# A four-block transformer on one core: the projection with activations in two 16-bit parts, and the front of a fifth chunk of tokens inside the attention

## The chip, the cores and the metric

The kernel runs on one core of one Trainium2 chip. The metric is the device time of the whole kernel in microseconds, the median of three runs.

## The reference, cut to what matters

The input is x of shape (4, 2048, 256), in 32-bit floats. Four blocks follow each other, each as x = x + layernorm(block(layernorm(x))):

```python
# block 1: softmax attention, 16 heads of 16, no projections (q, k: x times a row each)
attn = softmax(q @ k.T / 4) @ x_head
# block 2: mixes each token with the one ahead of it, then
out = sigmoid(xr @ W_r.T) * (square(relu(xk @ W_k.T)) @ W_v.T)
# block 3: linear attention with 8 heads, then its own MLP
x = x + msg;  x2 = layernorm(x, g2, be2)
h = gelu(x2 @ w1.T + b1)              # exact gelu, 1024 wide
x = x + (h @ w2.T + b2)               # the projection that the change is about
# block 4: gated MLP, 768 wide, integer weights
h = silu(x @ wg.T) * (x @ wu.T);  out = h @ wd.T
```

## The kernel before, in words

**Attention.** The first part of the program (`softmax_attention`) goes through 64 pairs of batch and head, called heads 0 to 63 here, eight of them to a group. A head is 16 key blocks j. For each, TensorE makes the scores (L468, 16-bit), ScalarE takes their exponential (L742, two instructions of 128x1024 a key block), and TensorE multiplies them with the values (L591). Scores are made three key blocks ahead, in three buffers of PSUM. At a head's end VectorE copies the sums out of PSUM (L894), and TensorE turns them (L641).

**The front inside the attention.** The tokens are handled in 16 chunks of 512 behind the attention, four chunks to a batch. Block 2 and the first half of block 3 of a chunk (norms, mixing, three matrix products of block 2, then k, v, q and the sums k times v of block 3) are its front. The fronts of the first `EARLY` = 4 chunks are done during the attention, from head 17 on, when the heads of batch 0 are there. A front is 17 pieces on TensorE (`PIECES`, two transposes of n, mix_r0 ... val1, two of u, k0 ... q1, kv), spread over steps, 18 to a chunk. Each piece uses the one spare bank of PSUM, is cut in two parts that stand three key blocks apart, and is read by VectorE before the next one may begin. `front_at` says behind which key blocks of a head pieces stand: at j = 2 in every head, and at j = 10 as well in odd heads and in the last group. So 68 pieces stand in heads 18 to 63: 23 heads hold two, 22 hold one. ScalarE does three extra instructions a chunk between its exponentials (L681, L684, L687), POOL (GpSimd) the inverse roots of the norms, and SyncE (SP) the loads and stores.

**The later layers.** `later_layers` does the rest as a pipeline over chunks. A stage of each chunk belongs to one of eight streams, and stream s works on chunk "iteration minus SHIFT[s]". Streams 0, 1 and 2 are the front of the chunks from `EARLY` on; l and m make the message of the linear attention and y; a does fc (L1514, y times w1, 48 products in 16 bits a chunk), the gelu (L1646, ScalarE, into hT in 32 bits) and the projection (L1378 with hT, 32 products in 32 bits a chunk, called proj0 to proj3); b the integer MLP's gate and up products (L1542) and the down products (L1558); c the output. Iterations 1 and 2 ("thin") hold 0, 1, 2, l and m alone; from iteration 3 on a is there, and from then to iteration 12 an iteration does all ("full"); in iteration 13 stream 2 is the last of the front's, and 14 to 20 are "drain". The order on each engine is written out by hand in `PE_ORDER`, `ACT_ORDER`, `DVE_ORDER`, `POOL_ORDER` and `SP_ORDER`, one list of stages for each phase. Engines take their queues in that order and wait on semaphores. PSUM banks 0 and 1, 2 and 3, 4 and 5 are shared between stages of different streams; 6 and 7 hold fc's products and the projection's. fc's product i waits until the gelu has read product i - 2 (`gelu_done`).

The lines that turn up below: `stats` and `norm` helpers L1744 to L1755 (VectorE), POOL's inverse root L1344 and its sum with the bias b2 L1354, x4's residual sum L1893, the transposes and splitting of w1 at L1450, L1705, L1708 and L1826, and VectorE's and ScalarE's two instructions for the parts of the gated product, L1920 and L1688.

## Time and profile before

| | us |
|---|---|
| median of three runs (3086.8 to 3090.0) | 3089.66 |
| the profiled execution | 3088.71 |
| its span, first to last instruction | 3086.4 |
| TensorE busy in it | 2866.7 |
| ScalarE busy | 2412.6 |
| VectorE busy | 1374.1 |

The span is what the profile accounts for; the profiled execution's own time lies 2.3 us above it. Busy times are sums over the whole span, and the two parts of the program have different limits, so the stretches have to be read one by one. The attention ends at about 1981 us.

### The profile page before, as it was taken

The page shows a single profiled execution, that of the slowest core. Times are in us where ns is not written, and L with a number is a line of the kernel's source. Part 1 is how long each engine was busy: PE and PEld are TensorE (multiplying, and loading weights), DVE is VectorE, ACT ScalarE, POOL GpSimd, SP SyncE. Part 2 cuts the span into 40 slices and gives each one's busy share as a digit, 9 for nine tenths or more (in the row PEclk, how much of TensorE's full clock was granted, in tenths as well). Part 3 has the DMA queues.
Part 4 walks back from the last instruction along what each step waited for, and adds up shares of the span by engine and source line. Part 5 has one row for each costly group of instructions (what it writes and reads, how often), then busy time and mean ns, then how long its engine had stood idle before and what let it go on. Part 6 is the DMA issues. An engine that isn't in the chain of part 4 may idle for free. (4 is left out here: it accounts for less than half of the span.)

```text
span 3086.4 us, 48514 instructions
## 1 busy us (share of the span) xinstructions
PE 2866.7 (93%) x18320; PEld 1153.1 (37%) x18320; DVE 1374.1 (45%) x3395; ACT 2412.6 (78%) x2681; POOL 223.8 (7%) x193
## 2 busy tenths in 40 slices
PE   3999999999999999999999999779999999999996
PEld 0221221222222222222222222256766666666664
DVE  5221220321432233223330142277778888865675
ACT  5999999999999999999999999654444444443432
POOL 0000000000000000000000000011111111211110
PEclk9999999999999999999999999889999999999998
DMA  3411111311210211111120111121222212111110
GB/s 119 153 36 37 64 39 37 100 43 33 76 57 25 83 62 55 52 50 40 59 74 25 37 52 43 39 75 55 63 82 68 61 61 76 61 48 51 38 48 22
DMA packets 125586, 177.51 MB, mean 58 GB/s; under 512 B 42248, under 2 KB 100616, under 8 KB 125128
## 3 DMA queue, kind: packets, MB, share of 16 engines
...
## 5 line engine op out<-in xcount | busy, mean ns | idle before, releaser
L742 ACT ACTIVATE probs<-ps 128x1024 f32<-128x1024 f32 x2048 | 1893.0, 1168 | 46.5 <-PE ps L468 45.7
L591 PE MATMUL ps<-probs,vals 128*32 128x512 f32 x8192 | 1092.2, 605 | 2.9 <-ACT probs L742 2.9
L468 PE MATMUL ps<-qT,kT 64*128 64x512 f16 x4096 | 728.4, 385 | 83.8 <-DMA kT<-split_dram 17.9
L468 PEld LDWEIGHTS ps<-qT,kT 64*128 64x128 f16 x4096 | 173.2, 93 | 1125.4 <-ACT probs L742 1030.8
L1680 ACT ACTIVATE gate<-layers_ps 128x512 f32<-128x512 f32 x96 | 57.3, 597 | 279.4 <-PE layers_ps L1542 157.4
L894 DVE COPY sums<-ps 128x512 f32<-128x512 f32 x64 | 44.3, 692 | 516.8 <-PE ps L591 516.8
L591 PEld LDWEIGHTS ps<-probs,vals 128*32 128x32 f32 x8192 | 161.5, 108 | 294.1 <-issue 228.8
L1378 PE MATMUL layers_ps<-weight_mem,hT 128*128 128x256 f32 x1024 | 230.8, 380 | 0.0
L1378 PEld LDWEIGHTS layers_ps<-weight_mem,hT 128*128 128x128 f32 x1024 | 193.0, 190 | 29.9 <-ACT hT L1646 1.2
L1514 PE MATMUL layers_ps<-yT,weight_mem 128*128 128x512 f16 x768 | 172.8, 379 | 13.6 <-ACT hT L1646 13.6
L1542 PE MATMUL layers_ps<-n4T,weight_mem 128*128 128x512 f16 x768 | 177.3, 384 | 6.7 <-DVE y_out L1755 4.3
L1646 ACT ACTIVATE hT<-layers_ps,weight_mem,fc_scale 128x512 f32<-128x512 f32 x128 | 95.3, 772 | 44.6 <-PE layers_ps L1514 44.4
L813 DVE TENSOR_SCALAR qk<-ps,q_factor 128x512 f32<-128x512 f32 x32 | 24.0, 750 | 223.3 <-PE ps L459 223.2
L1514 PEld LDWEIGHTS layers_ps<-yT,weight_mem 128*128 128x128 f16 x768 | 73.9, 98 | 100.4 <-ACT hT L1646 18.1
L1542 PEld LDWEIGHTS layers_ps<-n4T,weight_mem 128*128 128x128 f16 x768 | 75.8, 99 | 95.3 <-issue 11.5
L1913 DVE SCALAR_TENSOR_TENSOR gate<-layers_ps,gate 128x512 f32<-128x512 f32 x96 | 66.3, 690 | 68.5 <-PE layers_ps L1542 59.3
L1558 PE MATMUL layers_ps<-weight_mem,gated 128*128 128x256 f16 x768 | 88.1, 273 | 3.2 <-DVE gated L1920 3.2
L1378 PE MATMUL layers_ps<-weight_mem,uT 128*128 128x256 f32 x384 | 85.1, 379 | 0.6 <-issue 0.6
L1344 POOL TENSOR_TENSOR rstd_x<-ve_x,neghalf_k 128x4 f32<-128x4 f32 x55 | 62.9, 1144 | 294.0 <-DVE ve_x L1750 293.5
L1558 PEld LDWEIGHTS layers_ps<-weight_mem,gated 128*128 128x128 f16 x768 | 74.8, 98 | 18.5 <-issue 7.3
L1378 PEld LDWEIGHTS layers_ps<-weight_mem,uT 128*128 128x128 f32 x384 | 72.9, 190 | 12.0 <-issue 1.3
L1688 ACT ACTIVATE gated<-gate 128x512 f16<-128x512 f32 x96 | 60.0, 625 | 18.7 <-DVE gate L1913 18.6
...
## 6 DMA issues: line engine op xcount, KB each, us to landing
...
```

Of the source, the lines that this page charges most:

```text
L468: last = nc.tensor.matmul(SCORES[slot][:, n * BANK:(n + 1) * BANK], kT[buf][rows, j * P:(j + 1) * P], qT[buf][rows, q0:q0 + BANK], start=T ...
L591: mm = nc.tensor.matmul(ACC[32 * c:32 * c + 32, :], vals[buf][:, j, :], probs[:, j % PROBS, c * BANK:(c + 1) * BANK], start=(j == 0), stop ...
L742: nc.scalar.activation(probs[:, j % PROBS, half * T // 2:(half + 1) * T // 2], SCORES[slot_of(at)], ACT.Exp, scale=OPERAND_SCALE ** -2).th ...
L1344: pool.tensor_tensor(rstd[l][:, :], ve[l][:, :], neghalf[:, :], ALU.pow).then_inc(sem("rstd_" + l), 1)
L1378: last = nc.tensor.matmul(dst, x[:, k, blk * P:(blk + 1) * P], w[:, k, :], start=(k == 0), stop=(k == kk - 1))
L1514: last = nc.tensor.matmul(ps[:, 6 + i % 2, :], w1_parts[:, w, k, i * P:(i + 1) * P], yT16[:, y, k, :], start=((w, y, k) == products[0]), s ...
L1542: last = nc.tensor.matmul(ps[:, a + i, :], W16[w][:, k, m * P:(m + 1) * P], n4T16[:, p, k, :], start=(p == k == 0), stop=(p == 1 and k == ...
L1558: last = nc.tensor.matmul(dst, gated16[:, p, k, blk * P:(blk + 1) * P], W16["wd"][:, k, :], start=(p == k == 0), stop=(p == 1 and k == M2 ...
L1646: A(hT[:, i, :], ps[:, 6 + i % 2, :], ACT.Gelu, scale=fc_scale[:, i:i + 1], bias=W["b1"][:, 0, i:i + 1]).then_inc(sem("gelu_done"), 1)
L1680: A(gate[:, m % 2, :], ps[:, up_bank(m), :], ACT.Silu, scale=DEQUANT / NORM_SCALE if exact16 else DEQUANT).then_inc(sem("silu_done"), 1)
L1688: A(gated16[:, 0, m, :], gate[:, m % 2, :], ACT.Copy).then_inc(sem("gated_high"), 1)
L1913: V.scalar_tensor_tensor(dst, ps[:, up_bank(m) + 1, :], DEQUANT / NORM_SCALE * HIDDEN_SCALE if exact16 else DEQUANT, gate[:, m % 2, :], AL ...
```

## The change

**The projection.** hT now holds the activations in two 16-bit parts. ScalarE's gelu writes to a new tile `hidden` of four slots; a second ScalarE instruction for each of the eight blocks (stages hh0 to hh3, two blocks each) scales it and writes the high part; a VectorE instruction (hl0 to hl3) writes what is left of it as the low part and counts `h_done`. w2 is split in two 16-bit parts as well, by VectorE during the last group of the attention (`rows_of_fc`, with one more reduction over partitions on POOL). A block of the projection is then 24 products in 16 bits (high by high, high by low, low by high) in place of 8 in 32 bits. It waits for `h_done`, and the gelu waits for `h_done` too, three blocks back, because of the four slots. The orders of all engines are written anew for this.

**The fifth chunk.** `EARLY` is 5, and `front_at` gives (2, 10) for every head. 85 pieces stand in heads 18 to 62: two in each of them, except one in 19, 21 and 62 and none in 23. `SHIFT` changes with it: LEAD falls from 1 to 0, and the pipeline of the later layers has iterations 0 to 19, of which 0 holds the load of the message's input and the diagonal copy alone, 1 is the only thin one, 2 to 11 are full, 12 has stream 2 as the last of the front's, and 13 to 19 are drain. Splitting w1 and the integer weights moves into iteration 1. To make room, the tiles attn and x0 are laid over n1 and x1, so the next chunk's loads wait for `mix_mm`, `n1_done` and `x1_kept`.

```diff
@@ constants and the front's places
-EARLY = 4
+EARLY = 5
 def front_at(head):
-    return (2, 10) if head // GH + 1 == GROUPS or head % 2 else (2,)
+    return (2, 10)
@@ rows_of_fc (VectorE, last group)
+                if e == 3:
+                    fch.link(V.tensor_tensor(w2, w2, hidden_bound[:, :].unsqueeze(2).broadcast_to([P, M1, C]), ALU.mult))
+                    fch.link(V.tensor_reduce(widest_row[:, 0:1], w2.rearrange("p m c -> p (m c)"), AX.X, ALU.max, apply_absolute_value=True))
...
+                    fch.link(V.tensor_scalar(product, w2[:, m, :], widest_row[:, 0:1], PROJ_SCALE, ALU.mult, ALU.mult))
+                    fch.link(V.tensor_copy(parts[:, :, 0, :], product))
+                    fch.link(V.tensor_tensor(parts[:, :, 1, :], product, parts[:, :, 0, :], ALU.subtract))
@@ orders, one list of each engine's
 ACT_ORDER "all":
-fc0 mix fc1 fc2 uT mix_k fc3 nT mix_r up0 up1 high0 up2 high1 up3 high2 up4 high3 up5 high4 keep high5 ...
+fc0 hh0 mix fc1 fc2 hh1 uT fc3 mix_k hh2 nT keep hh3 mix_r up0 high0 up1 up2 high1 high2 up3 up4 high3 up5 high4 high5 ...
 POOL_ORDER "drain":
-x4 ffn b2 msg o
+b2 x4 ffn msg o
@@ later_layers
-        attn = sb("attn", [P, H, K4, D])
+        attn = fr_a[:, :, :].rearrange("p k c -> p (k c)").rearrange("p (h k d) -> p h k d", h=H, k=K4)
-        f = r_gate
+        x0, f = x1, r_gate
-        hT = sb("hT", [P, M1, N])
+        hT, hidden = sb("hT", [P, M1, N]), sb("hidden", [P, 4, N])
@@ load_in (SP)
                 sp.wait_ge(sem("x1_done"), c)
+                sp.wait_ge(sem("mix_mm"), c)
...
+                sp.wait_ge(sem("n1_done"), c)
+                sp.wait_ge(sem("x1_kept"), c)
@@ proj (TensorE)
-                    pe.wait_ge(sem("gelu_done"), c * M1 + M1)
-                    tok_out(blocks(6)[:, k, :], hT, k, W["w2"], M1).then_inc(sem("proj_mm"), 1)
+                    pe.wait_ge(sem("h_done"), c * M1 + M1)
+                    products = [(h, w, m) for h, w in ((0, 0), (0, 1), (1, 0)) for m in range(M1)]
+                    for h, w, m in products:
+                        last = nc.tensor.matmul(blocks(6)[:, k, :], h_parts[:, h, m, k * P:(k + 1) * P], w2_parts[:, w, m, :],
+                                                start=((h, w, m) == products[0]), stop=((h, w, m) == products[-1]))
+                    last.then_inc(sem("proj_mm"), 1)
@@ fc and h_high (ScalarE)
                     for i in range(part * M1 // 4, (part + 1) * M1 // 4):
                         act.wait_ge(sem("fc_mm"), c * M1 + i + 1)
-                        A(hT[:, i, :], ps[:, 6 + i % 2, :], ACT.Gelu, scale=fc_scale[:, i:i + 1], bias=W["b1"][:, 0, i:i + 1]).then_inc(sem("gelu_done"), 1)
+                        act.wait_ge(sem("h_done"), c * M1 + max(i - 3, 0))
+                        A(hidden[:, i % 4, :], ps[:, 6 + i % 2, :], ACT.Gelu, scale=fc_scale[:, i:i + 1], bias=W["b1"][:, 0, i:i + 1]).then_inc(sem("gelu_done"), 1)
...
+                        A(h_parts[:, 0, i, :], hidden[:, i % 4, :], ACT.Copy, scale=hidden_scale[:, i:i + 1]).then_inc(sem("h_high"), 1)
@@ h_low (VectorE)
+                        V.scalar_tensor_tensor(h_parts[:, 1, i, :], hidden[:, i % 4, :], hidden_scale[:, i:i + 1], h_parts[:, 0, i, :],
+                                               ALU.mult, ALU.subtract).then_inc(sem("h_done"), 1)
@@ o_layer (VectorE)
-                V.tensor_tensor(flat(o), wide(6, 2), flat(o), ALU.add).then_inc(sem("o_done"), 1)
+                V.scalar_tensor_tensor(flat(o), wide(6, 2), proj_scale[:, 0:1], flat(o), ALU.mult, ALU.add).then_inc(sem("o_done"), 1)
```

What the new orders do is seen in the order of the built programs. In the rows below, L numbers of the changed program are its own.

**TensorE, from the transposes of iteration 2 (before) to the first fc.** Before, iteration 1 stands ahead of these rows; L1366 turns n (fr_a), u and y, L1495 is the message, L1372 and L1378 are products in 32 bits, L1450 turns w1, L1514 is fc:

```order
L1366 MATMUL layers_ps<-ident,u 128x128 x8
L1495 MATMUL layers_ps<-kv_diag,q_in 128x132 x8
L1372 MATMUL layers_ps<-uT,weight_mem 128x512 x4
L1378 MATMUL layers_ps<-weight_mem,uT 128x256 x8
L1372 MATMUL layers_ps<-xk,weight_mem 128x512 x4
L1378 MATMUL layers_ps<-weight_mem,xr 128x256 x8
L1378 MATMUL layers_ps<-weight_mem,k_act 128x256 x8
L1450 MATMUL layers_ps<-ident,weight_mem 128x128 x8
L1378 MATMUL layers_ps<-weight_mem,uT 128x256 x8
L1366 MATMUL layers_ps<-ident,y 128x128 x8
L1484 MATMUL layers_ps<-v_ones,k_feat 128x130 x8
L1514 MATMUL layers_ps<-yT,weight_mem 128x512 x12
```

The changed program, from its very first instruction in the later layers to the first fc:

```order
L1483 MATMUL layers_ps<-ident,weight_mem 128x128 x8
L1395 MATMUL layers_ps<-ident,fr_a 128x128 x8
L1528 MATMUL layers_ps<-kv_diag,q_in 128x132 x8
L1407 MATMUL layers_ps<-weight_mem,xr 128x256 x8
L1483 MATMUL layers_ps<-ident,weight_mem 128x128 x8
L1401 MATMUL layers_ps<-xk,weight_mem 128x512 x4
L1407 MATMUL layers_ps<-weight_mem,k_act 128x256 x8
L1395 MATMUL layers_ps<-ident,y 128x128 x8
L1547 MATMUL layers_ps<-yT,weight_mem 128x512 x12
```

The products with uT (q, v and k) and v_ones of an iteration are gone ahead of the first fc, and so is a whole round of transposes, xk, xr and k_act. Both halves of w1 are turned in the one iteration that is left.

**ScalarE, in a full iteration, from the first gelu.** hT and hidden are the gelu's outputs, n1T, xk and xr belong to the mixing, uT to u:

```order
L1646 ACT_TABLE_LOAD
L1646 ACTIVATE hT<-layers_ps,weight_mem,fc_scale 128x512 x2
L1585 ACTIVATE n1T<-layers_ps 128x2x512
L1591 ACTIVATE xk<-n1T,one_minus_mu 128x512 x2
L1591 ACTIVATE xr<-n1T,one_minus_mu 128x512 x2
L1646 ACTIVATE hT<-layers_ps,weight_mem,fc_scale 128x512 x4
L1609 ACTIVATE uT<-layers_ps,weight_mem 128x512 x2
L1601 ACTIVATE k_act<-layers_ps 128x1024
L1603 ACTIVATE k_act<-k_act 128x1024
L1646 ACTIVATE hT<-layers_ps,weight_mem,fc_scale 128x512 x2
L1654 ACTIVATE n4T<-layers_ps 128x1024
L1596 ACTIVATE r_gate<-layers_ps 128x1024
```

The changed program:

```order
L1682 ACTIVATE hidden<-layers_ps,weight_mem,fc_scale 128x512 x2
L1691 ACTIVATE hT<-hidden,hidden_scale 128x512 x2
L1622 ACTIVATE n1T<-layers_ps 128x2x512
L1628 ACTIVATE xk<-n1T,one_minus_mu 128x512 x2
L1628 ACTIVATE xr<-n1T,one_minus_mu 128x512 x2
L1682 ACTIVATE hidden<-layers_ps,weight_mem,fc_scale 128x512 x4
L1691 ACTIVATE hT<-hidden,hidden_scale 128x512 x2
L1646 ACTIVATE uT<-layers_ps,weight_mem 128x512 x2
L1682 ACTIVATE hidden<-layers_ps,weight_mem,fc_scale 128x512 x2
L1638 ACTIVATE k_act<-layers_ps 128x1024
L1640 ACTIVATE k_act<-k_act 128x1024
L1691 ACTIVATE hT<-hidden,hidden_scale 128x512 x2
```

Two copies of the high part (hT<-hidden) now stand between the first two gelus and the mixing, and two more after the sixth gelu.

**VectorE, in the first iteration that does x4, from x4's statistics on.** x4's end is ve_x, n4T is the low part of the next transposed input, r_gate is f:

```order
L1750 TENSOR_SCALAR ve_x<-mv_x 128x4
L1785 SCALAR_TENSOR_TENSOR xk<-n1T,weight_mem,xk 128x512 x2
L1785 SCALAR_TENSOR_TENSOR xr<-n1T,weight_mem,xr 128x512 x2
L1788 TENSOR_SCALAR n1T<-n1T,keep 128x2
L1755 TENSOR_SCALAR n<-x,mv_x,rstd_x 128x256 x4
L1744 BN_STATS stats_attn<-attn 128x6 x4
L1748 BN_AGGR mv_attn<-stats_attn 128x2 x4
L1750 TENSOR_SCALAR ve_attn<-mv_attn 128x4
L1903 SCALAR_TENSOR_TENSOR n4T<-layers_ps,n4T 128x1024
L1793 SCALAR_TENSOR_TENSOR r_gate<-r_gate,layers_ps 128x1024
```

The changed program:

```order
L1795 TENSOR_SCALAR ve_x<-mv_x 128x4
L1930 SCALAR_TENSOR_TENSOR hT<-hidden,hidden_scale,hT 128x512 x2
L1830 SCALAR_TENSOR_TENSOR xk<-n1T,weight_mem,xk 128x512 x2
L1830 SCALAR_TENSOR_TENSOR xr<-n1T,weight_mem,xr 128x512 x2
L1833 TENSOR_SCALAR n1T<-n1T,keep 128x2
L1930 SCALAR_TENSOR_TENSOR hT<-hidden,hidden_scale,hT 128x512 x2
L1800 TENSOR_SCALAR n<-x,mv_x,rstd_x 128x256 x4
L1956 SCALAR_TENSOR_TENSOR n4T<-layers_ps,n4T 128x1024
L1930 SCALAR_TENSOR_TENSOR hT<-hidden,hidden_scale,hT 128x512 x4
L1838 SCALAR_TENSOR_TENSOR r_gate<-r_gate,layers_ps 128x1024
```

Eight low parts (hT<-hidden,hidden_scale,hT) stand in three places, the statistics of attn go behind f, and the last four low parts stand behind n4T.

## Rows read from the trace of the kernel before

**Rows 1.** the page: span, and busy tenths of three engines in 40 equal slices
```profile
span 3086.4 us, 48514 instructions
...
PE   3999999999999999999999999779999999999996
...
DVE  5221220321432233223330142277778888865675
ACT  5999999999999999999999999654444444443432
```

**Rows 2.** windows in the attention: head 14, heads 17-63, head 40, 41, 31, 56-63
```profile
core 0: us, PE busy (x) PEld busy (x) DVE busy (x) ACT busy (x) POOL busy (x), PEclk, DMA share, GB/s
469.98:499.31 29.33, 27.60 (x198) 5.92 (x196) 1.57 (x5) 29.33 (x34) 0.00 (x0) 1.00 0.10 32
558.44:1978.58 1420.14, 1375.00 (x9728) 336.87 (x9726) 416.38 (x885) 1400.75 (x1514) 34.74 (x33) 1.00 0.16 52
1248.59:1278.31 29.72, 28.94 (x210) 7.14 (x206) 12.14 (x23) 29.17 (x32) 0.00 (x0) 1.00 0.18 60
1278.31:1309.03 30.72, 30.59 (x218) 8.47 (x218) 8.35 (x15) 30.23 (x34) 0.00 (x0) 1.00 0.17 57
975.28:1007.59 32.31, 30.59 (x210) 7.50 (x210) 3.75 (x7) 31.36 (x35) 0.00 (x0) 1.00 0.09 32
1735.34:1978.58 243.24, 236.87 (x1672) 59.87 (x1668) 69.73 (x140) 237.70 (x256) 8.61 (x6) 1.00 0.12 39
```

**Rows 3.** groups by line: work of a front piece on TensorE
```profile
L516 PE MATMUL ps<-weight_mem,fr_xr 128*128 128x256 f32 x128 | 36.2, 405 | 0.0
L560 PE MATMUL ps<-fr_uT,weight_mem 128*128 128x512 f32 x32 | 18.0, 645 | 0.0
```

**Rows 4.** windows in the later layers, from one first fc matmul to the next
```profile
2020.70:2062.80 42.10, 33.03 (x144) 26.62 (x145) 35.17 (x103) 18.06 (x20) 6.14 (x7) 0.82 0.26 75
2062.80:2121.60 58.80, 53.38 (x251) 39.73 (x249) 38.79 (x124) 21.24 (x25) 10.36 (x9) 0.97 0.28 81
2473.60:2544.40 70.80, 68.41 (x355) 48.38 (x353) 57.74 (x158) 33.44 (x43) 12.89 (x10) 1.00 0.22 67
2864.50:2909.80 45.30, 43.94 (x242) 29.64 (x240) 32.01 (x86) 18.92 (x25) 6.36 (x5) 1.00 0.13 46
```

**Rows 5.** groups by line: the projection, down products, high and low halves
```profile
L1378 PE MATMUL layers_ps<-weight_mem,hT 128*128 128x256 f32 x1024 | 230.8, 380 | 0.0
L1558 PE MATMUL layers_ps<-weight_mem,gated 128*128 128x256 f16 x768 | 88.1, 273 | 3.2 <-DVE gated L1920 3.2
L1688 ACT ACTIVATE gated<-gate 128x512 f16<-128x512 f32 x96 | 60.0, 625 | 18.7 <-DVE gate L1913 18.6
L1920 DVE TENSOR_TENSOR gated<-gate,gated 128x512 f16<-128x512 f32 x96 | 65.5, 686 | 14.3 <-ACT gated L1688 12.8
```

**Rows 6.** timelines (start us, us long) of TensorE and VectorE at the start of the later layers
```profile
1988.51 1.94 PE L1366 MATMUL layers_ps<-ident,fr_a 128*128 128x128 f32 x8 [8.53 <-issue]
2009.97 1.22 DVE L1793 SCALAR_TENSOR_TENSOR r_gate<-r_gate,layers_ps 128x1024 f32<-128x1024 f32 x1 [4.78 <-PE layers_ps L1378]
2029.93 0.17 DVE L1859 TENSOR_SCALAR denom<-layers_ps 128x16 f32<-128x16 f32 x1 [0.54 <-PE layers_ps L1495]
2060.01 2.28 DVE L1826 TENSOR_TENSOR weight_mem<-gated,weight_mem 128x2048 f16<-128x2048 f32 x1
2062.85 1.43 PE L1514 MATMUL layers_ps<-yT,weight_mem 128*128 128x512 f16 x5
```

**Rows 7.** timeline of TensorE in a full iteration
```profile
2482.95 5.35 PE L1514 MATMUL layers_ps<-yT,weight_mem 128*128 128x512 f16 x24 [1.05 <-ACT hT L1646]
```

**Rows 8.** timelines of VectorE and GpSimd: x4's sum, in the full iteration, then drain
```profile
2478.55 3.37 DVE L1893 TENSOR_TENSOR x<-x_in,x 128x1024 f32<-128x1024 f32 x1
2478.48 2.35 POOL L1354 TENSOR_TENSOR o<-x,row_mem 128x1024 f32<-128x1024 f32 x1 [4.89 <-DVE x L1755]
...
2867.26 1.23 DVE L1893 TENSOR_TENSOR x<-x_in,x 128x1024 f32<-128x1024 f32 x1
```

141 lines of the change are left out of this document (88 added, 53 removed).

## The prediction, made before the changed kernel was run

> **What bounds the kernel now.** I read the page's slices first, to see that the program has two parts [rows 1]. In the first 25 or so of the 40 slices TensorE and ScalarE are both at nine tenths or more; behind them TensorE alone is, with VectorE at seven to eight tenths and ScalarE at four. So each part needs its own table by stretches.
>
> In the attention a window is one head, from one copy of the sums to the next [rows 2]. Head 14, with no piece of the front, takes 29.33 us, and ScalarE is busy for all of it: its 32 exponentials set the pace, while TensorE has 29.33 - 27.60 = 1.7 us to spare. Head 40, with one piece, takes 29.72 us with TensorE busy for 28.94. Head 41, with two, takes 30.72 with TensorE busy for 30.59: it has become the bound. Over heads 17 to 63 the time is 1420.1 us, and 47 heads of 29.33 would be 1378.5: the 68 pieces cost 41.6 us.
>
> In the later layers a window is one iteration, from its first fc product to the next one's [rows 4]. A full iteration takes 70.8 us with TensorE busy for 68.4 and VectorE for 57.7; one of the drain takes 45.3 with TensorE busy for 43.9, VectorE for 32.0. TensorE bounds both; VectorE idles 13.1 and 13.3 us.
>
> **The change, part by part.**
>
> *Front in the attention.* Twenty-two heads with a single piece cost about 0.39 each (head 40), 8.6 in all. The other 41.6 - 8.6 = 33.0 us belong to the 23 heads with two: 1.43 each. Now 41 heads hold two and three hold one: 41 x 1.43 + 3 x 0.39 = 59.8 us, which is **18 us more**. The eight last heads have stood next to each other with two pieces already (one only in head 63): 243.24 - 8 x 29.33 = 8.6 us for 15 pieces, 1.15 a pair, so pairs in neighbouring heads don't pile up there. That is the low end: 48 us, a rise of 7. The dearest pair (head 31, 32.31 us) cost 2.98; 41 of them would be 122 us, a rise of 81. I take 1.43, since it is the mean of 23 cases and lies near head 41's. The fifth chunk's work is far more than that: 12 of a chunk's 17 pieces stand in four groups, two of 36.2 us and two of 18.0 for four chunks, one of each shown [rows 3], so 27 us a chunk, and most of it lies in TensorE's spare time. VectorE's new instructions for w2 stand in the last group of heads, where it is busy for 69.7 of 243.2 us [rows 2], and go at nothing. They handle some ten times 128x1024, and at x4's 1.23 us each [rows 8] they would be 12 us if that cover were gone.
>
> *A thin iteration less.* Before, TensorE's first instruction in the later layers is at 1988.5 and the first fc at 2062.85 [rows 6], 74.3 us for two iterations in which TensorE idles much; the second takes 42 us [rows 4]. The changed order on TensorE has one such iteration left. In it VectorE is the chain, up to w1's low part, which fc needs. In the old second iteration VectorE is busy for 35.2 us [rows 4]; of that n2, u, q_feat, k_feat and the last norm of n1 (some 6.5 us, at 1.2 to 1.4 for each pass over 128x1024) now stand behind the low part or are gone, which leaves 28.7. The old window idles for another 6.9; I keep half, 3.3. Ahead of it TensorE needs 6.5 us for w1, n and the message, the last of them 3.1 at the clock of these iterations (its granted share is 0.82 there [rows 4]); the old order let mixing and message overlap with other work, as the heads of f, of the message and of the low part show [rows 6]. That is 38.5 us to the first fc. 74.3 - 38.5 = 36; I take **35 us less**, with 28 and 40 as ends. The exponential and splitting work of the dropped iteration is the fifth chunk's and is hidden in the attention, as priced above.
>
> *The projection on TensorE.* A chunk's 64 records of the 32-bit product take 230.8/1024 x 64 = 14.4 us by the group and 13.8 by start times; 96 in 16 bits, at the down product's 88.1/768 = 0.115 (0.108 by start times), take 11.0 or 10.4 [rows 5]. That is 3.4 us less a chunk.
>
> *What it adds elsewhere.* Per chunk eight copies on ScalarE (0.625 us, like L1688) and eight two-input instructions on VectorE (0.69, like L1920; 0.62 from start to start in a row), 5.0 us each [rows 5]. In a full iteration VectorE has 57.7 + 5.0 = 62.7 us to do, 65.4 with the waits inside its norm chains, and TensorE 68.4 - 3.4 = 65.0: they are **level**, so a full iteration cannot fall by 3.4. I walked one with these durations. The first joint is fc's: the gelu of product 4 comes 1.25 us later, because two copies of the high part stand ahead of the mixing on ScalarE, so fc2 waits some 2.3 us where it waited 1.05 [rows 7]. The second is at n4: the last low parts and n4_low sit close behind each other, and f and the first up product wait half a microsecond. The third is k_feat, where VectorE waits for ScalarE's exponential and then keeps kv, q and the next fc behind it. The walk closes at 68.4 us: **2.4 less**, for nine iterations that hold streams a and 1 in full, 21.6 us.
>
> In the drain TensorE has 43.9 - 3.4 = 40.5 us of work. The projection now waits for the last low part: eighth gelu, two copies of 0.6, two low parts of 0.6, where it waited for nothing; about 1.6 us of the gain go there. A further one is POOL's. In a full iteration x4's sum takes 3.37 us while POOL adds b2 (2.35 us) beside it, and 1.23 in the drain, where POOL does so later [rows 8]. The new order puts b2 first in the drain too, so x4's sum grows by 2.1 us there and hands some 1 us on to the low parts and the projection. The Trainium skill says the same (GPSIMD Engine Reference, its table's row on SBUF interfaces: shared with VectorE, contention with instructions that have two SBUF inputs); the trace agrees by these two rows. By that rule the low parts, with two SBUF inputs, would be slowed as well wherever they meet b2. Without any such meeting the drain would be 4 us shorter in all than I say. I take 43.6 us an iteration, **1.7 less**, for four: 6.8. The iteration with a but no b saves 2.5, the one with stream 2 last 2.3, and the last chunk's 1.5. Together the 16 projections save 21.6 + 6.8 + 6.3 = **34.7 us**, of 54 that TensorE's work alone would give. SP's new waits cost nothing: the attn load now starts behind the transpose of n, some 4 us into an iteration, and is wanted after 30; x0's is wanted after 60. Without that cover, a load's 5.5 to 6.4 us.
>
> **The sum.** Span: 3086.4 + 18 - 35 - 34.7 = 3034.7 us; the profiled execution's own time 3088.71 - 51.7 = 3037.0, and the median of the runs stands 0.95 above it: 3038.
>
> **The rivals.**
> - *TensorE stays the bound throughout*: VectorE's 13 us of idle time swallow the 5.0 whole. 16 x 3.4 = 54 instead of 34.7: 3019. For it is that the idle time is there; against it, that VectorE waits only where it must.
> - *VectorE binds and the full iterations gain nothing*: 21.6 us less of gain, 3060. For it: 65.4 us of chain in 70.8 leave little, and the queue is strictly in order, so each wait for POOL's roots adds.
> - *Slower: VectorE keeps all its waits.* They are for POOL, ScalarE and TensorE and may simply shift. A full iteration is then 57.7 + 5.0 + 13.1 = 75.8 us, 5.0 more, and the drain's 50.3; with 5 us more in 16 iterations, 80 in place of a gain of 34.7, the time is 3038 + 115 = 3153. It ends slower as soon as an iteration is longer by (35 - 18)/16 = 1.1 us on average. Against it: most of these waits are for TensorE, whose work shrinks.
> - *Pairs pile up in the attention*, each as dear as head 31's: 63 us more, 3101. It takes 2.7 us a pair to lose all the gain. Against it are the last eight heads.
> - *The change doesn't shorten the pipeline's start*: some other chain (the late loads, the 8 us of copies for the integer weights on ScalarE) holds the first fc for 15 us more: 3053.
>
> **How the numbers follow.** Forecast 0.58; TensorE bound throughout 0.11; full iterations without gain 0.16; a late start 0.07; piled pairs 0.04; VectorE's waits kept 0.03; 0.01 for something else. About 0.2% (6 us) is what a measurement of this kernel can tell from no change. All cases but the two slower ones are over 6 us faster: faster 0.91, within 0.2% 0.02 (either slow mechanism half way), slower 0.07. Low end: TensorE bound with the low price of the front, near 3010; I cut at 3014. High end: no gain in full iterations, with a few microseconds more in the attention: 3064. Outside lie about 0.15.
>
> **What would show it.** Right: heads with two pieces at 30.5 to 31 us, and the last head's sums at about 1997 instead of 1978.6; the first fc near 2046 (18 later, 35 earlier); full iterations at 68.4 with VectorE busy for about 63; the drain at 43.6; x4's sum near 3.4 in the drain. Wrong: full iterations at 67.4 or below with TensorE never waiting (first rival), or at 70.8 and more with TensorE waiting for VectorE (second and third), heads at 32 (fourth), or a first fc past 2060 (fifth).

## The result, and the profile after

Over its runs the changed kernel takes 3069.12 us (median of 4, 3066.76 to 3071.46), the kernel before 3089.18 (3086.8 to 3090.0): a ratio of 0.9936, 95% interval 0.9924 to 0.9948. It is faster by 20 us. The forecast was 3038 with 3014 to 3064 as its range, so the direction was right and the size was not. The profiled execution took 3067.5 us, its span is 3065.7.

The page of the changed kernel, span and the same three rows of the 40 slices as in [rows 1]:

```profile
span 3065.7 us, 50078 instructions
...
PE   3999999999999999999999999958999999999996
...
DVE  5221230323433432433241152157998989976886
ACT  5999999999999999999999999954455555554543
```

In the last 14 slices VectorE went from seven and eight tenths to eight and nine, and ScalarE from four to five. TensorE still shows nines. The slices don't tell which of the two is waited for.

Windows of the changed kernel, with the columns of [rows 2]: heads 17 to 63, head 40, the first iteration with fc, a full one, the first drain iteration and the third:

```profile
559.14:1991.63 1432.49, 1394.05 (x9840) 349.70 (x9838) 467.65 (x995) 1407.20 (x1517) 40.30 (x39) 1.00 0.17 54
1259.31:1290.01 30.70, 30.42 (x210) 6.80 (x208) 13.61 (x27) 29.85 (x33) 1.11 (x1) 1.00 0.36 100
...
2041.90:2106.60 64.70, 54.90 (x280) 38.22 (x281) 45.86 (x132) 30.86 (x35) 11.39 (x10) 0.89 0.21 65
2523.60:2593.60 70.00, 65.38 (x387) 45.36 (x385) 62.99 (x165) 38.29 (x52) 13.16 (x11) 1.00 0.22 67
2792.00:2842.70 50.70, 44.60 (x275) 27.90 (x273) 40.49 (x95) 25.81 (x35) 6.87 (x5) 0.93 0.19 63
2889.70:2935.00 45.30, 41.05 (x275) 26.64 (x273) 39.37 (x94) 23.44 (x33) 6.86 (x5) 1.00 0.14 46
```

Read against [rows 2] and [rows 4]:

| stretch (iterations cut at their first fc product) | before | after | difference | forecast |
|---|---|---|---|---|
| to the last head's sums | 1978.6 | 1991.6 | +13.0 | +18 |
| from there to the first fc product | 84.3 | 50.3 | -34.0 | -35 |
| the first iteration with fc | 58.8 | 64.7 | +5.9 | -2.5 |
| the ten after it, to the drain | 697.0 | 685.4 | -11.6 | -23.9 |
| four iterations of the drain | 183.0 | 189.7 | +6.7 | -6.8 |
| last chunk, to the end | 84.8 | 84.0 | -0.8 | -1.5 |
| from the first fc product to the end | 1023.6 | 1023.8 | **+0.2** | **-34.7** |

The two parts of the change at the front came out nearly as priced. The projection in two parts gained nothing: TensorE's work in a full iteration fell by 3.0 us where 3.4 were forecast (68.41 to 65.38), VectorE's rose by 5.25 (57.74 to 62.99), and the iteration fell from 70.8 us to 70.0 only. TensorE, which waited for 2.4 us of an iteration, now waits for 4.6.

What it waits for in that full iteration, from the view of waits (engine, line, releaser: us in total, times, longest):

```profile
PE layers_ps L1395 <- DVE n L1800: 1.3, 1, 1.3
PE layers_ps L1547 <- ACT hidden L1682: 1.2, 1, 1.2
PE layers_ps L1395 <- DVE q L1880: 1.1, 1, 1.1
...
PE layers_ps L1407 <- DVE y_out L1800: 0.8, 1, 0.8
```

The second and the third were there before ([rows 7] has one). The first and the last are new: TensorE waits for VectorE's norm of n4, and mix_r then waits for y_out's norm to give banks 4 and 5 back.

### The profile page after: what moved, and what is told of

Its sections match the earlier page's. It is cut to its first block and busy times, and to the rows that moved or that the text cites. A ratio compares the mean times of both kernels' runs of the same rounds, so it can differ in the third digit from the quotient of the medians.

```text
span 3065.7 us, 50078 instructions
## 1 busy us (share of the span) xinstructions
PE 2820.9 (92%) x18832; PEld 1101.8 (36%) x18832; DVE 1491.9 (49%) x3565; ACT 2481.5 (81%) x2796; POOL 233.4 (8%) x194
## 5 line engine op out<-in xcount | busy, mean ns | idle before, releaser
L471 PE MATMUL ps<-qT,kT 64*128 64x512 f16 x4096 | 719.2, 385 | 74.7 <-DMA kT<-split_dram 18.9
L1547 PE MATMUL layers_ps<-yT,weight_mem 128*128 128x512 f16 x768 | 181.3, 390 | 31.7 <-ACT hidden L1682 20.9
L1557 PE MATMUL layers_ps<-weight_mem,hT 128*128 128x256 f16 x1536 | 180.4, 277 | 11.1 <-DVE hT L1930 11.1
L1557 PEld LDWEIGHTS layers_ps<-weight_mem,hT 128*128 128x128 f16 x1536 | 152.2, 99 | 37.8 <-DVE hT L1930 12.3
L1682 ACT ACTIVATE hidden<-layers_ps,weight_mem,fc_scale 128x512 f32<-128x512 f32 x128 | 94.3, 771 | 56.5 <-PE layers_ps L1547 34.7
L1930 DVE SCALAR_TENSOR_TENSOR hT<-hidden,hidden_scale,hT 128x512 f16<-128x512 f32 x128 | 89.1, 746 | 22.4 <-ACT hT L1691 22.4
L1691 ACT ACTIVATE hT<-hidden,hidden_scale 128x512 f16<-128x512 f32 x128 | 84.9, 712 | 2.0
```

The costliest lines, as they stand in the source:

```text
L471: last = nc.tensor.matmul(SCORES[slot][:, n * BANK:(n + 1) * BANK], kT[buf][rows, j * P:(j + 1) * P], qT[buf][rows, q0:q0 + BANK], start=T ...
L1547: last = nc.tensor.matmul(ps[:, 6 + i % 2, :], w1_parts[:, w, k, i * P:(i + 1) * P], yT16[:, y, k, :], start=((w, y, k) == products[0]), s ...
L1557: last = nc.tensor.matmul(blocks(6)[:, k, :], h_parts[:, h, m, k * P:(k + 1) * P], w2_parts[:, w, m, :], start=((h, w, m) == products[0]), ...
L1682: A(hidden[:, i % 4, :], ps[:, 6 + i % 2, :], ACT.Gelu, scale=fc_scale[:, i:i + 1], bias=W["b1"][:, 0, i:i + 1]).then_inc(sem("gelu_done"), 1)
L1691: A(h_parts[:, 0, i, :], hidden[:, i % 4, :], ACT.Copy, scale=hidden_scale[:, i:i + 1]).then_inc(sem("h_high"), 1)
L1930: V.scalar_tensor_tensor(h_parts[:, 1, i, :], hidden[:, i % 4, :], hidden_scale[:, i:i + 1], h_parts[:, 0, i, :], ALU.mult, ALU.subtract). ...
```

## The loop behind the full iteration

From these waits I formed **theory A**, of which the expectations below speak. An iteration's length is set neither by TensorE's work nor by VectorE's, but by a loop made of stretches of both:

1. VectorE works with no gap above 0.4 us from k_feat to the norm of y_out (k_feat, y_low, in1, kv, diag, in2, q_feat, x4, the first two pairs of low parts, mix, ffn, n4, y_out).
2. That norm frees banks 4 and 5 for TensorE's mix_r; from mix_r on TensorE works without a gap to the end of v and k.
3. ScalarE takes the k features (one pass, a table, one exponential), and VectorE's k_feat follows.

The projection's products stand in stretch 2, and half of its new low parts (hl0, hl1) in stretch 1. So the change takes from the one and gives to the other. The joints, in timelines (start us, us long): first VectorE and TensorE in the kernel before,

```profile
2465.42 1.23 DVE L1831 SCALAR_TENSOR_TENSOR k_feat<-layers_ps,k_feat 128x1024 f32<-128x1024 f32 x1
2490.68 1.90 DVE L1755 TENSOR_SCALAR y_out<-layers_ps,mv_ffn,rstd_ffn 128x256 f32<-128x256 f32 x4
2492.72 3.69 PE L1378 MATMUL layers_ps<-weight_mem,xr 128*128 128x256 f32 x16
2536.21 1.23 DVE L1831 SCALAR_TENSOR_TENSOR k_feat<-layers_ps,k_feat 128x1024 f32<-128x1024 f32 x1
```

then the same in the changed kernel, with the start of v and k:

```profile
2515.46 1.23 DVE L1876 SCALAR_TENSOR_TENSOR k_feat<-layers_ps,k_feat 128x1024 f32<-128x1024 f32 x1 [1.12 <-ACT k_feat L1666]
2543.22 1.90 DVE L1800 TENSOR_SCALAR y_out<-layers_ps,mv_ffn,rstd_ffn 128x256 f32<-128x256 f32 x4
2545.26 3.69 PE L1407 MATMUL layers_ps<-weight_mem,xr 128*128 128x256 f32 x16 [0.81 <-DVE y_out L1800]
2574.89 7.07 PE L1407 MATMUL layers_ps<-weight_mem,uT 128*128 128x256 f32 x32
2585.42 1.22 DVE L1876 SCALAR_TENSOR_TENSOR k_feat<-layers_ps,k_feat 128x1024 f32<-128x1024 f32 x1 [1.09 <-ACT k_feat L1666]
```

mix_r starts as y_out's norm ends, in both kernels: 2490.68 + 1.90 = 2492.58 and 2543.22 + 1.90 = 2545.12. The loop set the pace of the kernel before as well, but only just: TensorE's wait at this joint was too short to be listed, and experiment 2 shows that its own way from k_feat to mix_r was 0.3 us shorter than VectorE's. Cut at these starts, the stretches are, in one full iteration of each (the runs of the lower rows come below):

| kernel | k_feat to mix_r | mix_r to v, k | v, k to k_feat | sum |
|---|---|---|---|---|
| before | 27.30 | 32.96 | 10.53 | 70.79 |
| changed | 29.80 | 29.63 | 10.53 | 69.96 |
| b2_late | 27.67 | 30.12 | 10.53 | 68.32 |
| diag_moved | 28.82 | 29.65 | 10.53 | 69.00 |
| more_in | 32.59 | 31.06 | 10.53 | 74.18 |
| more_out | 29.68 | 31.31 | 10.54 | 71.53 |
| fifth_only | 27.28 | 32.95 | 10.53 | 70.77 |
| before_b2_late | 27.02 | 34.02 | 10.53 | 71.57 |
| best | 27.28 | 30.32 | 10.53 | 68.13 |

The three columns add up to the iteration whatever bounds it, because they are cuts of it. What can speak for A is which column an edit moves, and by how much.

The change took 3.3 us from the second column and put 2.5 into the first. Two more things stood in the first column already: x4's sum, 3.4 us because GpSimd adds b2 beside it, and diag. So A says where gain is to be had, and the experiments try it.

## The experiments

Each line with times has the ratio to the kernel before, measured on the same chip, with its 95% interval.

**1. The two halves apart.** proj_only keeps the projection and takes the fifth chunk's front back out of the attention; fifth_only is the changed kernel with the 32-bit projection.

```diff
-EARLY = 5
+EARLY = 4
...
-    return (2, 10)
+    return (2, 10) if head // GH + 1 == GROUPS or head % 2 else (2,)
```

> The changed kernel with EARLY = 4 and front_at as before, so the projection in two 16-bit parts alone, with the new orders. Theory A (chained loop: a full iteration is VectorE's unbroken stretch from k_feat to y_out's norm, then TensorE's from mix_r to k, then 3.4 us of ScalarE; the projection takes 3.4 us from TensorE's part and adds 2.5 us of low parts to VectorE's): full iterations about 70.0 us, nothing gained over all, 3086 to 3090 us. Theory B (the projection does bring its gain, and the fifth chunk brings less than the pipeline's shorter start shows): full iterations still 70, but the whole 20 us or more faster than before, near 3065.

```diff
-                    pe.wait_ge(sem("h_done"), c * M1 + M1)
-                    products = [(h, w, m) for h, w in ((0, 0), (0, 1), (1, 0)) for m in range(M1)]
...
+                    pe.wait_ge(sem("gelu_done"), c * M1 + M1)
+                    tok_out(blocks(6)[:, k, :], hT, k, W["w2"], M1).then_inc(sem("proj_mm"), 1)
```

> The changed kernel with the projection as before (32-bit, no high and low parts, no splitting of w2), so the fifth chunk alone, with the new orders without the stages hh and hl. Theory A: the fifth chunk gives all of the gain, first fc near 2042, full iterations near 70.6, drain 45.3; 3063 to 3070 us, no slower than the changed kernel. Theory B: 3085 us or more.

fifth_only: 3068.59 us (ratio 0.9934, 0.9917 to 0.9951), the same as with the projection. The whole gain of the change is the fifth chunk's. Beside fifth_only the new projection makes the ten iterations 10 us shorter (685.4 for 695.3), the first 2.7 longer, the last chunk 1.2 shorter, and the four of the drain 7.3 longer (189.7 for 182.4). In fifth_only TensorE's granted clock is 1.00 in all four; in the changed kernel it is in one of them only.

proj_only: 3104.98 us (1.0053, 1.0036 to 1.0070), 16 us slower than before and outside what I expected. From the first fc product to the last chunk's it is 7.0 us shorter than before (931.7 for 938.7), and the last chunk 2.8 longer. The loss is in the start: the last head's sums stand within 0.7 us of before, and the first fc product comes 18.9 us later, at 2081.8 instead of 2062.85. The timeline of TensorE in proj_only shows the wait ahead of it:

```profile
2078.19 3.80 PE L1517 MATMUL layers_ps<-v_ones,k_feat 128*128 128x130 f32 x16 [17.78 <-DVE k_feat L1876]
```

The changed thin order fits one thin iteration, and proj_only has two; the k features then stand behind keep_x1 and w16's 8 us of copies. Two kernels try whether that, and not the projection, makes the start late: one moves w16 alone behind the k features, the other gives the thin iterations their orders of the kernel before.

```diff
-    "thin": "w1a mix uT v q_low q w1b mix_k mix_r yT keep_x1 w16 k_low k".split(),
+    "thin": "w1a mix uT v q_low q w1b mix_k mix_r yT keep_x1 k_low k w16".split(),
```

> The kernel with the projection's half alone (3105), with one thing changed: in ScalarE's thin order w16's 8 us of copies stand behind the k features' two passes. If the 19 us that its first fc came late were those of the start (VectorE's k_feat waited 9.2 us for the exp behind w16, and k, v and q feature work behind it), the first fc comes 5 to 15 us earlier than 2081.8 and the time is 3090 to 3100, the full iterations staying at 69.8. If the loss lay in the iterations, nothing changes: 3105.

```diff
-    "thin": "w1a mix msg uT q v mix_r w1b mix_k val k yT kv".split(),
+    "thin": "w1a mix uT msg q v mix_k mix_r val w1b k yT kv".split(),
...
-    "thin": "w1a mix uT v q_low q w1b mix_k mix_r yT keep_x1 w16 k_low k".split(),
+    "thin": "w1a w16 mix uT v q_low mix_k q mix_r w1b k_low yT k keep_x1".split(),
...
-    "thin": "diag mix msg in0 y in1 q_feat f y_low x2 k_feat w1_low kv in2 n2 u".split(),
+    "thin": "diag mix msg in0 in1 y q_feat f x2 y_low k_feat in2 w1_low n2 kv u".split(),
...
-    "thin": "msg in0 in1 f x2 n2".split(),
+    "thin": "in0 msg f in1 x2 n2".split(),
```

> The kernel with the projection's half alone, with the thin iterations' orders of the kernel before (w1's second half and w16 where they were). If its loss of 16 us is that of the start, the first fc comes at 2060 to 2068 for 2081.8, the rest stays (fc to fc 932 us), and the time is 3082 to 3092. If the projection itself costs, it stays above 3097.

proj_only_w16: 3102.69 us (1.0032, 1.0017 to 1.0047), first fc at 2077.3. That is 4.5 us earlier, less than expected: keep_x1, which waits for x2's sum, still stands ahead of the k features on ScalarE. Its five runs lie between 3091.9 and 3103.5 us, the widest of all kernels here, and the two fastest are those with the highest granted clock (0.986 and 0.985 for 0.983), so its time tells little beside its trace. proj_only_start: 3092.76 us (1.0011, 1.0002 to 1.0021), 0.8 above what I expected, first fc at 2071.4 (2060 to 2068 expected), and 932.5 us from there to the last chunk's. So 10 of the 19 us were the orders. The other 8.5 stand in proj_only_start's trace, in one wait of VectorE: diag, which the changed order puts at the head of a thin iteration, waits there for the products of the message ahead of it.

```profile
2033.70 0.18 DVE L1894 COPY kv_diag<-kv_sums 32x64 f32<-32x64 f32 x1 [8.33 <-PE layers_ps L1528]
```

In the kernel before diag stood at the end of a thin iteration, and ran without a wait. No run moves it back, so for these 8.5 us the cause is read from the trace and not tried. proj_only and proj_only_start agree on what the projection does from the first fc on in a program with the old front: 6 to 7 us less up to the last chunk, 1 to 3 more in it, 4 to 5 in all where 34.7 were forecast.

**2. b2 off the path.** In the changed kernel GpSimd's order begins with b2, which meets x4's sum in stretch 1. Here it stands behind f, and behind ffn in the drain.

```diff
-    "all": "b2 x4 ffn f msg x2 n2 o in0 in1".split(),
+    "all": "x4 ffn f b2 msg x2 n2 o in0 in1".split(),
...
-    "drain": "b2 x4 ffn msg o".split()}
+    "drain": "x4 ffn b2 msg o".split()}
```

> The changed kernel with POOL's sum with b2 put behind the root for f in full iterations and behind ffn's root in the drain, so that it no longer runs beside x4's sum. Theory A: x4's sum takes 1.23 instead of 3.37 us, and as it stands in VectorE's stretch of the loop, full iterations fall by about 2 us to 68, drain by up to 2: 3040 to 3050 us. Theory C (the limit is VectorE's total work and POOL is not in it, or the wait moves to another pair): full iterations stay within 0.5 us of 70, over 3062 us.

3058.14 us (0.9897, 0.9880 to 0.9913). x4's sum, in the timelines of VectorE in the changed kernel and of b2_late:

```profile
2528.68 3.37 DVE L1946 TENSOR_TENSOR x<-x_in,x 128x1024 f32<-128x1024 f32 x1
```

```profile
2525.47 1.23 DVE L1946 TENSOR_TENSOR x<-x_in,x 128x1024 f32<-128x1024 f32 x1
```

The sum is 2.1 us shorter, the first stretch too (29.80 to 27.67), and the full iteration 1.7, because the second stretch takes 0.5 more. By the trace b2 has a price in its new place too: it runs beside a VectorE instruction of 4 columns (L1795), which takes 0.77 us for 0.17, and TensorE waits 0.3 us for the gate product behind it. In the first two of the ten iterations stretch 1 gets no shorter (31.3 to 31.8 us and 27.1 to 27.1), and both are 0.8 us longer; in the last the clock fell (0.92 for 0.97). So the ten give only 4.1 us together (681.3 for 685.4), and the four of the drain 7.9 (181.8 for 189.7). Most of these 7.9 are the clock's and one gelu's: an iteration of the drain at a granted clock of 1.00 takes 45.3 us in the changed kernel and 44.9 here. The gain came out at 11 us where I had expected 19 to 29.

The same move in the kernel before, as a cross:

```diff
-    "all": "b2 x4 ffn f in0 x2 n2 msg o in1".split(),
+    "all": "x4 ffn f in0 b2 x2 n2 msg o in1".split(),
```

> The kernel before with POOL's sum with b2 put behind the root for attn in full iterations (the drain had it late already). Theory A: before, TensorE never waits behind x4's sum (its two waits are for q_feat and for the gelu), so full iterations stay at 70.8 within 0.3 and the time at 3089 within 3 us. If x4's sum was on the path there as well: 68.7 a full iteration, near 3070 us.

3100.73 us (1.0036, 1.0023 to 1.0048): slower, and outside my expectation. x4's sum fell to 1.22 us here as well, but b2 met another instruction. From its timelines, GpSimd, VectorE and TensorE:

```profile
2511.95 2.43 POOL L1354 TENSOR_TENSOR o<-x,row_mem 128x1024 f32<-128x1024 f32 x1
2512.70 2.81 DVE L1755 TENSOR_SCALAR x<-r_gate,mv_f,rstd_f 128x256 f32<-128x256 f32 x4
2521.20 2.04 PE L1495 MATMUL layers_ps<-kv_diag,q_in 128*128 128x132 f32 x16 [0.90 <-DVE gate L1913]
```

The norm in the middle took 1.37 us in the kernel before. The delay reaches the up products' read and the message, inside stretch 2, which is 1.1 us longer. Stretch 1 is only 0.3 us shorter (27.30 to 27.02), though x4's sum is 2.1 us shorter, so the full iteration is 71.6 us, 0.8 longer. The reason stands at the joint of this iteration, in VectorE's and TensorE's timelines of before_b2_late:

```profile
2495.84 1.90 DVE L1755 TENSOR_SCALAR y_out<-layers_ps,mv_ffn,rstd_ffn 128x256 f32<-128x256 f32 x4
2499.41 3.62 PE L1378 MATMUL layers_ps<-weight_mem,xr 128*128 128x256 f32 x16
```

y_out's norm ends at 2497.74, and mix_r starts 1.7 us later without a wait, straight behind TensorE's own products. TensorE's own way from k_feat to mix_r, its waits for q's features and a gelu included, takes 27.0 us. So in the kernel before the two ways were level within 0.3 us: a shorter VectorE stretch could give it no more than that, while new VectorE work in it would lengthen stretch 1 in full. The cross shows as well that a move of b2 has its price wherever it lands.

**3. The same work inside and outside the stretch.** Four more instructions a chunk, two behind each of hl0 and hl1 (more_in), or behind each of hl2 and hl3 (more_out, where the first line's pair is (2, 3)). spare is a tile of 128x512 in 16 bits that nothing reads:

```diff
+                    if part in (0, 1):
+                        for again in range(2):
+                            dve.wait_ge(sem("spare_done"), c * 4 + part % 2 * 2 + again)
+                            V.scalar_tensor_tensor(spare[:, :], W["akv"][:, 0, :], hidden_scale[:, 0:1], W["akv"][:, 1, :], ALU.mult, ALU.subtract).then_inc(sem("spare_done"), 1)
```

> The changed kernel with four more VectorE instructions of 512 columns a chunk (about 0.7 to 0.8 us each with its wait, some 3 us a chunk, into a tile that nothing reads), two behind each of hl0 and hl1, inside the stretch from k_feat to the norm of y_out. Theory A (a loop of two stretches, VectorE from k_feat to the norm of y_out and TensorE from mix_r to the end of k, sets the full iteration): the full iteration goes from 70.0 to about 73 us, the time by 27 to 32 us in nine to ten iterations, and by 0 to 12 in the drain: 3096 to 3112. Rival (VectorE's total work sets it): the same here. Rival (TensorE sets it, 65 us busy of 70): at most +1 an iteration, under 3080.

> The same four instructions, but behind hl2 and hl3, outside that stretch, where VectorE waits 1.5 us for TensorE's value product and 0.4 and 0.7 us around it. Theory A: the full iteration stays within 0.7 us of 70.0; in the drain, where the projection waits for hl3, up to 3 us a chunk in four chunks: 3069 to 3088. Rival (total work): full iteration about 73, as in the other kernel, 3096 to 3112.

more_in: 3110.5 us (1.0066, 1.0049 to 1.0083), full iteration 73.2 to 74.5. more_out: 3092.18 us (1.0009, 0.9999 to 1.0019), full iteration 71.5. The times stand 41 and 23 us above the changed kernel, and the second is above what A expected. VectorE's and TensorE's work is the same in both, in one full iteration of each (more_in first):

```profile
2541.80:2616.00 74.20, 67.00 (x386) 46.50 (x385) 65.73 (x169) 38.56 (x51) 13.00 (x11) 0.98 0.21 64
```

```profile
2537.50:2609.00 71.50, 66.95 (x386) 46.59 (x385) 65.75 (x169) 38.40 (x51) 13.11 (x11) 0.98 0.21 66
```

Equal work and 2.7 us of difference: total work on VectorE can't be the bound, and the place decides. The table of stretches shows where: in more_in the first column is 2.8 us longer (29.80 to 32.59), in more_out 0.1 shorter. But both have 1.4 to 1.7 us more in the second column, which A did not foresee. TensorE is busy for 1.6 us more there with the same products. mix_r's 16 matmuls take 5.38 us in more_out where they took 3.69, and the windows around them give the reason (PEclk is the third number from the end; mix_r is the second row):

```profile
2557.10:2559.00 1.90, 1.09 (x8) 0.86 (x8) 1.86 (x5) 1.87 (x3) 0.00 (x0) 1.00 0.00 0
2559.00:2564.30 5.30, 5.25 (x17) 4.32 (x18) 4.58 (x6) 4.00 (x6) 0.00 (x0) 0.68 0.00 0
```

The granted clock is 0.68 over mix_r, partly at 1.2 GHz and partly at 2.4. In the changed kernel it is 1.00 there, as this window shows:

```profile
2545.20:2548.80 3.60, 3.54 (x17) 3.15 (x18) 2.92 (x3) 3.60 (x6) 0.00 (x0) 1.00 0.00 0
```

Before both, TensorE had nearly the same waits: 1.2 to 1.3 us, the transposes of n4 (1.1 us), and 0.8 us. Taking the clock off, the four instructions cost 2.8 us inside (0.7 each), all of it in the first column. Outside they are not free either. mix_r's clock fell in four full iterations of more_out; in others it stayed at 1.00, and there TensorE waits ahead of the second up product, for 2.8 us in the first two of the ten iterations and for 0.9 in the next two. By the orders it waits for the bank that VectorE's f, now later, gives back. One of these two:

```profile
2344.93 3.69 PE L1408 MATMUL layers_ps<-weight_mem,xr 128*128 128x256 f32 x16 [0.81 <-DVE y_out L1801]
2354.74 1.89 PE L1580 MATMUL layers_ps<-n4T,weight_mem 128*128 128x512 f16 x8 [0.93 <-issue]
```

The second column is 30.82 us there, 1.2 above the changed kernel's, and the iteration 71.1. Where mix_r is slow its 1.7 us hide that wait. So the same work costs 2.8 us inside and 1.2 outside at a granted clock of 1.00: it finds some 1.6 us of room outside and none inside. The half of A that these kernels test stands, that VectorE's place decides and not its total. Its expectation for more_out, within 0.7 us of 70.0, failed by the clock and, where the clock held, by stretch 2, which is not TensorE's alone.

**4. Work moved out of the stretch, none added.** diag's small copies go from between kv and in2 to behind y_out's sum, an iteration later.

```diff
-STAGES = {"0": "load_in in0 in1 in2 keep_x1", "1": "mix mix_r mix_k val f x2 n2 u", "2": "uT k k_low k_feat v q q_low q_feat kv", "l": "load_msg diag w1a w1b w1_low w16", "m": "msg y yT y_low",
+STAGES = {"0": "load_in in0 in1 in2 keep_x1", "1": "mix mix_r mix_k val f x2 n2 u", "2": "uT k k_low k_feat v q q_low q_feat kv", "l": "load_msg w1a w1b w1_low w16", "m": "diag msg y yT y_low",
...
-    "all": "x4 hl0 mix ffn hl1 b2 n4 out n4_low hl2 hl3 f up0 in0 low0 up1 up2 low1 low2 up3 x2 msg up4 low3 y up5 low4 n2 low5 o u k_feat y_low in1 kv diag in2 q_feat".split(),
+    "all": "x4 hl0 mix ffn hl1 b2 n4 out diag n4_low hl2 hl3 f up0 in0 low0 up1 up2 low1 low2 up3 x2 msg up4 low3 y up5 low4 n2 low5 o u k_feat y_low in1 kv in2 q_feat".split(),
```

> The changed kernel with the 16 small copies of the message's block diagonal (diag, 1.4 us with the wait ahead of it) moved on VectorE from between kv and in2 to behind y_out's sum, one iteration later, where VectorE waits for the high part of n4T. No work is added or removed. Theory A (the stretch of VectorE from k_feat to the norm of y_out is a part of the loop): it is 1.4 us shorter, so the full iteration falls from 70.0 to about 68.6, and the time by 10 to 18 us: 3051 to 3059. Rival (VectorE's total work, or TensorE's, sets it): 70.0 and 3069 as before, since both are unchanged.

3063.05 us (0.9917, 0.9901 to 0.9934), full iteration 69.0. The stretch is shorter by 1.0, not 1.4, since in2 now comes ahead of GpSimd's root, in VectorE's timeline:

```profile
2519.90 1.38 DVE L1800 TENSOR_SCALAR fr_a<-fr_x,mv_x,rstd_x 128x256 f32<-128x256 f32 x4 [0.60 <-POOL rstd_x L1373]
```

6 us came of it, for 10 to 18 expected, with the same sign as A and against both rivals, by which nothing should have moved.

**5. The way down from there.** In b2_late the start still had TensorE waiting for w1's low part. b2_thin computes it ahead of f, where VectorE waited, and copies w16 ahead of keep_x1:

```diff
-    "thin": "w1a mix uT v q_low q w1b mix_k mix_r yT keep_x1 w16 k_low k".split(),
+    "thin": "w1a mix uT v q_low q w1b mix_k mix_r yT w16 keep_x1 k_low k".split(),
...
-    "thin": "diag mix msg in0 y in1 q_feat f y_low x2 k_feat w1_low kv in2 n2 u".split(),
+    "thin": "diag mix msg in0 y in1 w1_low q_feat f y_low x2 k_feat kv in2 n2 u".split(),
```

> The best version (b2_late, 3058) with the thin iteration's orders changed: VectorE computes w1_low ahead of f, in a wait of 5.4 us, and ScalarE copies w16 ahead of keep_x1, in waits. TensorE's first fc, which waited 10.8 us for w1_low, comes 5 to 7 us earlier (2036 to 2038 for 2043), and the clock may not fall there. If the first full iteration passes it on, 3050 to 3054; if it waits for the gelus or for n1 instead, 3058 as before.

3050.47 us (0.9874, 0.9857 to 0.9890), with the first fc product at 2035.7. It waits 3.8 us where it waited 10.8, in the changed kernel and then in b2_thin:

```profile
2041.94 4.74 PE L1547 MATMUL layers_ps<-yT,weight_mem 128*128 128x512 f16 x12 [10.81 <-DVE weight_mem L1871]
```

```profile
2035.72 2.75 PE L1547 MATMUL layers_ps<-yT,weight_mem 128*128 128x512 f16 x12 [3.83 <-DVE yT L1923]
```

The same 12 products take 2.75 us instead of 4.74; the clock granted over the slow ones is 0.57, so TensorE was at its 1.2 GHz level for most of them.

best adds diag's move to b2_thin, and gelu_first then takes hh0 and hl0 out of the gelus' way:

> The same move in the best version (b2_thin, 3050.5), where the full iteration is 68.3 and TensorE waits 1.17 us for q's features and 1.16 for a gelu. By A the first wait goes and the second stays or shrinks: full iteration 66.5 to 67.5, time 3036 to 3045. If TensorE's other waits take the place, 3048 to 3052.

```diff
-    "all": "fc0 hh0 mix fc1 fc2 hh1 uT fc3 mix_k hh2 nT keep hh3 mix_r up0 high0 up1 up2 high1 high2 up3 up4 high3 up5 high4 high5 v k_low k yT keep_x1 q_low q".split(),
+    "all": "fc0 mix fc1 hh0 fc2 hh1 uT fc3 mix_k hh2 nT keep hh3 mix_r up0 high0 up1 up2 high1 high2 up3 up4 high3 up5 high4 high5 v k_low k yT keep_x1 q_low q".split(),
...
-    "all": "x4 hl0 mix ffn hl1 b2 n4 out diag n4_low hl2 hl3 f up0 in0 low0 up1 up2 low1 low2 up3 x2 msg up4 low3 y up5 low4 n2 low5 o u k_feat y_low in1 kv in2 q_feat".split(),
+    "all": "x4 mix hl0 ffn hl1 b2 n4 out diag n4_low hl2 hl3 f up0 in0 low0 up1 up2 low1 low2 up3 x2 msg up4 low3 y up5 low4 n2 low5 o u k_feat y_low in1 kv in2 q_feat".split(),
```

> The kernel 'best' (3054.3, full iteration 68.1) with ScalarE's first high parts hh0 (1.3 us) moved behind the gelus of fc1, VectorE's hl0 moved behind mix with them, and in the drain diag moved behind out. In 'best' TensorE's only large wait in the full iteration is 2.2 us of fc2 for the gelus of fc1, which stand behind hh0 and n1T's five passes on ScalarE. If that wait is ScalarE's chain, the gelus come 1.2 us earlier and the full iteration is 66.8 to 67.2, the drain again 45, the time 3035 to 3045. If a slot of hidden (gelu 4 waits for hl0, now later) or n1's chain takes its place, the full iteration stays at 68 and the time is 3050 to 3054.

best: 3054.25 us (0.9888, 0.9872 to 0.9905), full iteration 68.1, above both of its expectations. The wait for q's features went, and that of fc2 for ScalarE's gelus grew from 1.2 to 2.2 us; the drain lost 3.6 us, where diag stood ahead of n4_low (gelu_first has it behind out, and still loses 1.7 of them). gelu_first: 3050.29 us (0.9874, 0.9858 to 0.9891), full iteration 68.4. The gelus of fc1 come earlier, and the next one waits instead for a slot of hidden, which hl0 now gives back later, from ScalarE's and TensorE's timelines of gelu_first:

```profile
2523.55 1.45 ACT L1682 ACTIVATE hidden<-layers_ps,weight_mem,fc_scale 128x512 f32<-128x512 f32 x2 [1.33 <-DVE hT L1930]
2524.38 2.76 PE L1547 MATMUL layers_ps<-yT,weight_mem 128*128 128x512 f16 x12 [1.24 <-ACT hidden L1682]
```

In best mix_r no longer waits for y_out (TensorE reaches it 0.6 us behind the norm), so VectorE's stretch 1 is off the path there. By the waits that are left a second loop holds below 68.3 us, through ScalarE: gelu, high part, n's five passes, gelu, low part, slot. No run opens it, so it is argued and not shown; more slots for hidden were not tried. b2_thin and gelu_first are level and beat both kernels of the case by 1.3% and 0.6%.

## Why the prediction was wrong

By its own steps; 3034.7 forecast for the span and 3065.7 measured leave 31.0 us. The front in the attention made it 5.0 better than forecast and the thin iteration 1.0 worse. The other 34.9 lie behind the first fc product, where the projection was to bring 34.7 us and nothing came: 8.4 in the first iteration with fc, 12.3 in the ten after it, 13.5 in the drain, 0.7 in the last chunk.

- *Front in the attention, +18*: measured +13.0, of which 12.35 in heads 17 to 63 (1432.49 for 1420.14) and 0.7 earlier. The 85 pieces cost 54.0 us, (54.0 - 3 x 0.39)/41 = 1.29 a pair for 1.43. Head 40 with two takes 30.70, as head 41 did [rows 2]. The mechanism was right and the term 5 us too large. The rival of piled pairs didn't come.
- *A thin iteration less, -35*: measured -34.0. Right. That w1's low part would be the end of that chain showed as a wait of 10.8 us.
- *TensorE's projection, 3.4 less a chunk*: right, 68.41 to 65.38 by busy time and 3.3 in stretch 2.
- *The full iteration walked to 68.4*: **this is the step that failed**, at "I walked one with these durations". Measured 70.0. It began from "TensorE bounds both", read from 68.4 busy of 70.8, and set VectorE's 65.4 us against TensorE's 65.0 as sums over the whole iteration. VectorE's stretch 1 had no room: it was 27.3 us long, and TensorE needed 27.0 for the same way (before_b2_late), so the 2.5 us of low parts that were put there had to show in full. TensorE's 2.4 us of idle time, nearly all of them at VectorE's and ScalarE's joints, could have pointed there. With the loop cut at k_feat and mix_r, rows that were at hand give 27.3 + 2.5 for stretch 1 and 3.3 less for stretch 2: 70.0. The walk also looked at fc2, n4 and k_feat, but not at y_out's norm, which frees mix_r's banks. That b2_late, another kernel, came out at the walk's 68.4 (68.3) is chance.
- *GpSimd's b2*: priced at about 1 us in the drain and nowhere else. In a full iteration x4's sum had taken 3.37 us before [rows 8], so it brought nothing new, but it lies in the stretch that counts: 1.7 us a steady full iteration, shown by b2_late. In the drain x4's sum did grow to 3.4 us, but an iteration at a granted clock of 1.00 is only 0.4 us shorter without it, not 1.
- *The drain, 43.6*: measured 45.3 to 50.7, 189.7 us for four where 174.4 were forecast. This is the second step that failed, "about 1.6 us of the gain go there". At a granted clock of 1.00 an iteration takes 45.3 us, what it took before: TensorE's work fell from 43.9 to 41.1, and its idle time rose by as much, 2.3 us of it for the last low parts. In three of the four the clock fell behind that wait as well. One such place, in TensorE's timeline and in the window over it, and the same products in the iteration that kept its clock:

```profile
2857.34 7.08 PE L1557 MATMUL layers_ps<-weight_mem,hT 128*128 128x256 f16 x48 [2.27 <-DVE hT L1930]
```

```profile
2857.30:2864.30 7.00, 6.96 (x49) 5.62 (x50) 6.11 (x15) 1.33 (x2) 1.01 (x1) 0.76 0.00 0
```

```profile
2904.32 5.41 PE L1557 MATMUL layers_ps<-weight_mem,hT 128*128 128x256 f16 x48 [2.27 <-DVE hT L1930]
```

  The 1.7 us between are as much as an iteration of the drain was to gain in all, and no term of the drain had the clock. The first drain iteration (50.7) has a wait of 2.2 us for a gelu besides, with another 1.7 us lost to the clock behind it.
- *First iteration*, "saves 2.5": measured +5.9. fifth_only has 62.0 us there, so 3.2 are the new orders' around the start (its first gelu stands behind w16's copies and its first products at the low clock take 5.0 us), and 2.7 the projection's, where 2.5 less were forecast.
- *The rivals*: "VectorE binds and the full iterations gain nothing", 3060, was nearest, and what it said of the mechanism is half right. It is VectorE's chain, but by place and not by total work; 65.7 us of it fit into 71.5 where the added work stands outside the stretch. It had kept the drain's gain, which didn't come either; with that it would have been 3067. The other rivals didn't come.

The prediction had drawn on the Trainium skill (GPSIMD Engine Reference, its table's row on SBUF interfaces): contention of GpSimd with VectorE instructions "in a 2-port perf mode or with two SBUF inputs". The drain's x4 sum grew as it says, to 3.4 us. before_b2_late shows it for a norm as well, which has one tensor in SBUF and two scalars per partition: 1.37 us alone, 2.81 beside b2. By the page this would be the other half of its sentence, a 2-port mode; whether that mode was in force no run here shows.
